# Four-block graph network: adjacency load moved ahead of the turned group's swap, loops from round 3, all instruction lists rewritten

## What is computed

```
h = relu(layernorm(x));  x = x + GCN0(h, adj)        # 2 layers
h = relu(layernorm(x));  x = x + ATT1(h, adj + adj)  # 12 heads of 32
h = relu(layernorm(x));  x = x + ATT2(h, adj)
h = relu(layernorm(x));  x = x + GCN3(h, adj)        # 2 layers
...
GCN0 layer: u = h·(Wl h)'/√384 above and on the diagonal, h·(Wr h)'/√384 below;
            a = exp(u)·adj / row sum;   h = relu(LN(a @ (Wlin h + b)))
ATT:        p = softmax(q k'·scale + bias) per head;   out = (p v) Wo' + bo
GCN3 layer: a = softmax(h h'/√384)·adj / row sum;
            ctx = upper(a) @ (Wl h) + diag(a)·(Ws h) + lower(a) @ (Wr h);   h = relu(LN(ctx))
```

## Time and profile before

| | |
|---|---|
| median of three executions | 2807.22 us (2806.8 to 2807.78) |
| the profiled execution | 2810.98 us |
| its span, first to last instruction | 2809.2 us |
| mean granted TensorE clock | 0.988 |
| TensorE busy | 2684.6 us, 96% |
| VectorE, GpSimd, ScalarE busy | 78%, 53%, 44% |
| a round in the loop: GCN0, attention, GCN3 | 49.6, 33.3, 52.3 us |

### The profile page before, as it was taken

One profiled execution on the slowest core, in us unless ns is written; L12 is line 12 of the kernel. 1 busy time (PEld: TensorE's weight loads), 2 busy tenths in 40 slices (PEclk: granted clock), 3 DMA queues, 4 the chain that ended last, 5 costly groups with the idle time before them and its releaser, 6 DMA issues.

```text
span 2809.2 us, 85451 instructions
## 1 busy us (share of the span) xinstructions
PE 2684.6 (96%) x33582; PEld 2472.3 (88%) x33582; DVE 2184.4 (78%) x4130; ACT 1224.2 (44%) x2007; POOL 1495.1 (53%) x2499
## 2 busy tenths in 40 slices
PE   7999999999988999999989999998999999999997
PEld 7988888888878899999888999998888888888886
DVE  5776777767767788888877888888677777777776
ACT  3333333333333454544544545454444444444443
POOL 2222222223214566665544666665677777777776
PEclk9999999999999999999999999999999999999999
DMA  5332232322323433333353333333132222222221
GB/s 162 103 108 84 84 106 63 113 77 89 103 76 108 142 121 124 125 123 121 108 158 111 121 122 127 121 122 119 55 96 80 71 90 78 71 90 78 72 84 48
DMA packets 224451, 284.59 MB, mean 101 GB/s; under 512 B 18256, under 2 KB 203984, under 8 KB 224336
## 3 DMA queue, kind: packets, MB, share of 16 engines
q1 hardware_dynamic: 224336, 282.96, 32.1%
HBM read 182.62 MB, written 100.27 MB: 101 GB/s over the span
## 4 chain that ended last, share of the span: by engine, by line
PE 37%; issue 22%; DVE 16%; POOL 15%; DMA 5%; ACT 3%; SPq 2%; POOLq 0%; DVEq 0%; ACTq 0%
PE ps L373 27%; POOL wide L1610 7%; PE ps L1435 3%; PE ps L1417 3%; PE ps L1450 2%; DMA adjin<-in_adj 2%; DVE heads L1308 2%; DVE wide L1299 2%; DVE heads L1316 2%; DVE heads L1322 2%; DMA bounce<-xin 1%; POOL small L722 1%; DVE wide L1332 1%; POOL wide L1595 1%; PE ps L1965 1%
## 5 line engine op out<-in xcount | busy, mean ns | idle before, releaser
L373 PE MATMUL ps<-w_hi,split 128*128 128x384 f32 x4608 | 1271.6, 346 | 26.3 <-ACT split L1673 17.6
L373 PEld LDWEIGHTS ps<-w_hi,split 128*128 128x128 f32 x4608 | 849.1, 191 | 56.9 <-issue 17.8
L373 PE MATMUL ps<-split,w_hi 128*128 128x256 f32 x4608 | 863.4, 283 | 14.8 <-DVE w_lo L450 11.1
L373 PE MATMUL ps<-w_lo,split 128*128 128x384 f32 x2304 | 787.6, 342 | 0.0
L373 PEld LDWEIGHTS ps<-split,w_hi 128*128 128x128 f32 x4608 | 721.3, 189 | 32.2 <-ACT w_hi L439 11.3
L373 PE MATMUL ps<-split,w_lo 128*128 128x256 f32 x2304 | 584.7, 283 | 0.0
L373 PEld LDWEIGHTS ps<-split,w_lo 128*128 128x128 f32 x2304 | 435.7, 189 | 17.3 <-issue 17.3
L373 PEld LDWEIGHTS ps<-w_lo,split 128*128 128x128 f32 x2304 | 439.0, 191 | 1.3 <-issue 1.2
L731 POOL TENSOR_TENSOR rstd<-mv,pos_half 128x2 f32<-128x2 f32 x64 | 59.0, 923 | 569.3 <-DVE mv L926 569.3
L1187 POOL TENSOR_TENSOR wide<-wide 128x192 f32<-128x192 f32 x256 | 213.4, 865 | 252.1 <-ACT wide L1253 252.1
L1610 POOL TENSOR_TENSOR wide<-wide,row 128x192 f32<-128x192 f32 x512 | 315.7, 652 | 1.5 <-ACT wide L1686 1.5
(11 more groups left out here) (145 smaller groups left out, 4473.8 us busy)
## 6 DMA issues: line engine op xcount, KB each, us to landing
bounce<-xin SPq DMA_DIRECT2D x127, 384.0 KB, 3.1
wide<-bounce SPq DMA_DIRECT2D x508, 96.0 KB, 2.2
x_after<-wide SPq DMA_DIRECT2D x96, 384.0 KB, 2.5
wide<-x_after SPq DMA_DIRECT2D x96, 384.0 KB, 3.3
xin<-x_after SPq DMA_DIRECT2D x190, 192.0 KB
xin<-in_x SPq DMA_DIRECT2D x66, 192.0 KB
wide<-in_x SPq DMA_DIRECT2D x32, 384.0 KB, 4.4
out<-wide SPq DMA_DIRECT2D x32, 384.0 KB, 2.8
```

What stands on the lines that cost most here:

```text
L373: mm = nc.tensor.matmul(out, t if tokens_stay else w, w if tokens_stay else t, start=(k == 0), stop=(k == len(pairs) - 1))
```

## The change

No instruction's work is changed, and each stage runs as often as before. Three things are:

1. In `turn(i)`, `adjacency(s, i)` is issued before `swap_quarters(s, i)`, not behind `tokens(s, i + 1)`. With it, its wait for GpSimd stands ahead of SyncE's waits for the turned group.
2. `MIXED` is 3: each phase's loop runs rounds 3 to 15, and the straight code is a round per phase shorter (TensorE's program has 2979 rows of instructions instead of 3693).
3. The loop orders, `BEGINNING`, `BETWEEN` and `ENDING` of all engines are rewritten. Line numbers behind the lists are 36 lower.

```
@@ -21,223 +21,187 @@
-MIXED = 4
+MIXED = 3
...
 GCN3_ORDERS = [
...
-    "agg_0.1'' on_1.0'' adj_0.0' stat.1' diag_1.0'' on_1.1'' w0_1.0'' w1_1.0'' adj_1.0' w0_1.1'' w1_1.1'' "
-    "adj_0.1' diag_1.1'' adj_1.1' agg_1.0'' w0_0.0' on_0.0' w1_0.0' diag_0.0' z.0'' on_0.1' agg_0.0' "
-    "agg_1.1'' diag_0.1' w0_0.1' stat.0 w1_0.1' z.1''",
+    "adj_0.0' agg_0.1'' stat.1' on_1.0'' diag_1.0'' w0_1.0'' w1_1.0'' adj_1.0' adj_0.1' on_1.1'' adj_1.1' "
+    "w0_1.1'' w1_1.1'' diag_1.1'' agg_1.0'' w0_0.0' on_0.0' w1_0.0' diag_0.0' z.0'' on_0.1' agg_1.1'' "
+    "agg_0.0' diag_0.1' w0_0.1' stat.0 w1_0.1' z.1''",
...
     def turn(i):
         for s in range(STREAMS):
             store_and_reload(s, i - 2)
+            adjacency(s, i)
             swap_quarters(s, i)
             tokens(s, i + 1)
-            adjacency(s, i)
```

More of the change, by code:

```diff
@@ L29 @@
 BEGINNING = [
[29 rows of a table removed]
[19 rows of a table added]
 ]
 GCN0_ORDERS = [
[5 rows of a table removed]
[5 rows of a table added]
     "u_0.0' agg_1.1'' lin0_0.0' aT_0.0' lin1_0.0'",
[1 row of a table removed]
[1 row of a table added]
     "aT_0.0' z_1.1'' z_0.0' ml_0.1' norm.0 mr_0.1' hT_1.0' soft_0.1' aT_0.1' z_0.1' ml_1.0' mr_1.0' norm.1",
     "split_1.1'' soft_1.0'' att_1.0'' sum_1.0'' lin_1.0'' split_0.0' agg_1.0'' ln_1.0'' gain.0'' soft_1.1'' "
[2 rows of a table removed]
[2 rows of a table added]
     "agg_0.1' stat.1 ln_0.1' beta.1'' out.1'' turn.1",
[1 row of a table removed]
[1 row of a table added]
 ]
 ATT_ORDERS = [
-    "q0.1'' q1.1'' q2.1'' k0.1'' k1.1'' v0.1'' v1a.1'' pt0.0'' v1bc.1'' pt1.0'' pt2.0'' k2.1'' pv.0'' "
-    "scores.1'' out0.0'' out1.0'' q0.0' q1.0' q2.0' k0.0' k1.0' v0.0' v1a.0' pt0.1'' v1bc.0' pt1.1'' pt2.1'' "
-    "k2.0' pv.1'' scores.0' out0.1'' out1.1''",
-    "q.1'' pt0.0'' hT.0' pt1.0'' pt2.0'' k.1'' pv.0'' out.0'' norm.0 exp.1'' q.0' pt0.1'' hT.1' pt1.1'' "
+    "q0.1'' q1.1'' q2.1'' k0.1'' k1.1'' v0.1'' v1a.1'' pt0.0'' v1b.1'' pt1.0'' v1c.1'' pt2.0'' k2.1'' pv.0'' "
+    "scores.1'' out0.0'' out1.0'' q0.0' q1.0' q2.0' k0.0' k1.0' v0.0' v1a.0' pt0.1'' v1b.0' pt1.1'' v1c.0' "
+    "pt2.1'' k2.0' pv.1'' scores.0' out0.1'' out1.1''",
+    "q.1'' pt0.0'' hT.0' pt1.0'' pt2.0'' k.1'' pv.0'' norm.0 out.0'' exp.1'' q.0' pt0.1'' hT.1' pt1.1'' "
     "pt2.1'' k.0' pv.1'' out.1'' norm.1 exp.0'",
-    "abs.0'' fac.0'' v.1'' turn.1' stat.0 hT.0' pv.0'' s.1'' soft.1'' abs.1'' fac.1'' turn.0 stat.1 v.0' "
-    "hT.1' pv.1'' s.0' soft.0'",
-    "bias.1'' bias.0' p.0'' stat.0 out.0'' xb.1'' p.1'' stat.1 xb.0' out.1''",
+    "abs.0'' fac.0'' turn.1' hT.0' v.1'' stat.0 pv.0'' s.1'' soft.1'' abs.1'' fac.1'' turn.0 stat.1 hT.1' "
+    "v.0' pv.1'' s.0' soft.0'",
+    "bias.1'' bias.0' p.0'' stat.0 xb.1'' out.0'' p.1'' stat.1 xb.0' out.1''",
 ]
 GCN3_ORDERS = [
[4 rows of a table removed]
[4 rows of a table added]
     "on_0.0'' soft_0.1'' swap_0.1'' tiny_0.1'' w0_0.1'' w1_0.1'' hT_1.0'' norm.0' on_0.1'' w0_1.0'' "
[5 rows of a table removed]
[5 rows of a table added]
     "split_1.0' w2_0.1' ln_1.1'' turn.0 agg_0.1' out.1'' ln_0.1' soft_1.0' stat.1 att_1.0'",
[3 rows of a table removed]
[3 rows of a table added]
 ]
```

## The result

The changed kernel takes 2791.49 us (median of four, 2788.18 to 2795.12) against 2807.08 us before (median of four). The ratio is 0.9944, 95% interval 0.9927 to 0.9962: 15.6 us faster, where 38 were forecast. The profiled execution has a span of 2793.2 us, 16.0 less than before, so the trace shows the whole difference.

A forecast was written before the change was run, and what follows sets the result against it. TensorE, busy 2684.6 of 2809.2 us, was taken as the bound. The terms −22 − 9 − 18 + 2 + 0 + 9 = −38 us took the median of 2807 to 2769 us, range 2748 to 2800 us.

The forecast's parts named there:

- GCN3 loop, −22: GCN3 loop: earlier adjacency load and new order save 1.6 us in each of 14 rounds; bounds −28 and −5.
- B and C: GCN3 loop: TensorE's layer-1 aggregation waits for POOL's w0 and DVE's w2 rows; 1.2 us per round together, −0.9 forecast.
- A: GCN3 loop: TensorE's product waits for ACT's swap split; the new POOL order takes 0.70 us out of its 0.93.
- rival (2): GCN3 loop: waits are replaced, DVE comes last for w2; −5 instead of −22, 2786 us; chance 0.09.
- (3): First passage gains nothing, the stagger trades one chain for another; 2787 us; chance 0.09.
- (4): Loops cost, straight code doesn't: each of four added loop rounds brings a 2.1 us gap; 2786 us; chance 0.05.
- Attention, −9: Attention straight code: two fewer groups with gaps save 7 us, separated blocks at the second passage 2 us.
- First passage, −18: GCN0 to attention: staggered streams cut 39.5 us of gaps and lost clock to 21 to 23; bounds −25 and 0.
- Steady loops, 0: GCN0 and attention loops each gain a round that ran as straight code; no change, within 3 us either way.
- Start, +9: Start: late first product, +1.6, and waits after the first two aggregations, about 5, plus half clock; bounds +4 and +13.
- Third passage +2, end 0: Attention to GCN3 costs +2 us (−5 to +7); the last aggregations at the end stay, 0.
- Slower rival (5): GCN3: POOL's masks, now first, delay everything behind if the adjacency is late; about 2820 us at 7.3 us; chance 0.08.

The follow-up runs named there:

- e3: The changed kernel with DVE's out of stream 0 put back behind the normalise ln_0 in GCN3; 2792.61 us.
- e15: The kernel before with the early adjacency load and DVE's out of stream 0 moved ahead of ln_0 in GCN3; 2789.6 us, ratio 0.9917.
- e6: The changed kernel with rounds 3 and 4 of both attention phases written out as straight code; 2808.45 us.
- e11: The kernel before, late load and old orders kept, with only MIXED = 3, so loops start from round 3; 2802.87 us, ratio 0.9981.
- e1: The kernel before with one edit, the adjacency load issued ahead of the swap; 2778.36 us, ratio 0.9892.
- e12: The kernel before with the early adjacency load and POOL's GCN3 order as changed; 2791.4 us, ratio 0.9926.
- e5: The changed kernel with DVE's GCN0 order as before, straight code set to match; 2783.31 us, ratio 0.9909.
- e2: The changed kernel with the adjacency load put back behind the tokens' load; 3054.75 us, ratio 1.0877.

## Why the prediction was wrong

The miss of 22 us is as large as the error of one term, the GCN3 loop. The errors of the others cancel: the start and the GCN0 loop (5.3 and 4.3 us) and the first passage (4.7) came out dearer than forecast, the attention loops (6.5), the second and third passage and the end (2.3, 2.7, 2.5) cheaper. That is luck.

**GCN3 loop, −22: failed, at its second step.** That POOL's wait for the late adjacency is the cause of B and C held: the load alone takes 1.45 us off a round, against 1.6. The failing step is "of B and C together −0.9, since I don't know that the reordered DVE list keeps all of it", and the 0.70 for A. I priced the load on the old lists and treated the new lists as at worst a small deduction. They replaced A, B and C by a wait for the normalise (1.14 per round) and one for the split (0.52), and the round came out at −0.19. (The 0.70 for A came from a power moved ahead. That isn't what ended A: in e3 it is back at 1.14 per round with that power still ahead, and in e15, with the old place of the power, it is gone. It goes where hT waits instead.) The bound of −5 and rival (2), the waits are replaced and DVE comes last, had this, though DVE comes last with the normalise and the split and not with w2; its sign, a round of 52 with DVE as the releaser, is what the trace shows. At 2786 it is, with (3) and (4), 5 us from the result, and I gave it 0.09, with the argument that DVE idles where it waits for POOL. DVE's idle time says nothing of the order in which DVE comes to a piece of work, nor of what its instructions do to POOL's. The prediction said of A that POOL's second power leaves the chain; it did not look at which DVE instruction would now stand ahead of the normalise, and run beside the first.

**Attention, −9: right** in place and size for the second passage, −11.3. The price per group was too high (3.4; 1.4 to 2.1 by e6), the number of gaps closed too low: 4 rather than 2. `MIXED` alone gives it all (e11, −11.5 in its trace); the 2 us for the separated blocks show in no run.

**First passage, −18: size.** −13.3. The gaps that I had walked were there, a little longer (1.00 and 1.23 us at the last aggregations but one, 1.56 for the key copy, 1.73 for u, 2.91 at the pt transposes), and the clock is 0.90 in the middle, with 41.66 us of work, where over 44 and over 0.93 had been named as the sign. That the stagger of the streams made the gain isn't shown: no run has it alone. `MIXED` alone makes this passage 5.4 us shorter (e11), the early load alone 1 to 7 (e1, e12 to e15), and if the two add, the stagger has 1 to 7 of the 13.3 us.

**Steady loops, 0, within 3 either way: wrong in both** (+4.3 and −6.5). GCN0 lost 0.48 per round, to DVE's order (e5); attention gained 0.37 per round, where its TensorE had idled 0.2 to 0.4 in 50 us. No idle is left there:

```profile
1000.00:1050.00 50.00, 50.00 (x949) 48.79 (x951) 43.17 (x51) 25.54 (x37) 29.72 (x44) 1.00 0.39 125
```

I had the lists' differences before me and judged from TensorE's 0.2 to 0.4 us of idle that nothing could change. It bounds neither way. GCN0 lost more than it had idled, and attention gained twice its idle: over eight rounds (266.1 us before, 263.1 after) the idle fell by 1.5 us and the busy time of the same 4704 matmuls by another 1.5. Neither `MIXED` alone nor the load alone changes that round (33.24 to 33.34 us in e1 and e11), so the gain is that of the new attention lists; which word of them, no run shows.

**Start, +9: size.** +14.3, of which the forecast gaps are as said and 2.3 us of wait and some 2 of half clock were missed. **Third passage +2, end 0:** −0.7, within its bounds, and −2.5.

**Slower rival (5): didn't occur;** e2 shows what it would have cost. **Rival (4): no.** The time lies inside the range, 2748 to 2800 us, but the gain is 15.6 us where 38 were called likeliest.

## What to carry to other kernels

Price an edit on the lists that will run, not on those that ran: when a change moves one transfer and reorders everything, the transfer's gain can be had alone (here some 30 us of median for one line) and the orders must pay for themselves, stretch by stretch. Compare the two kernels by the start of the n-th group of a kind on the bound engine; the table says at once which lists to keep from which. Here the kernel put together so is 39 us under the changed one, though two of its parts missed by 9 and 7 us and cancelled. A small idle share of the bound engine in a steady loop says little: here one loop lost more than it had idled, and another gained twice as much, half of it out of the engine's busy time.

## What the runs showed of the hardware

- POOL's power on 128x2 takes 0.70 us, and 1.3 to 1.5 us when DVE's two-operand `out` (128x768, 0.95 us) has started before it or within 0.03 us after it: 29 of 64 with the new order. Where the power starts 0.07 to 0.10 us ahead of `out`, both take their usual time: 15 of 64 before. I had not expected it to be paid twice per round, nor that the time would hardly change when it was taken away (e3).
- A mask load that leaves behind the swap and the tokens again costs 263 us (e2), some 18 us in each of 13 rounds and the passage before them: where an in-order engine takes a piece of work first in its round, a late transfer costs its lateness in each round, and the clock falls too (0.86 in a window of the loop that is else at 1.00).
- The small matmuls of attention in code that runs once meet gaps with no releaser, in the second passage before seven of them, 14.6 us together; the same groups in a loop have none in 21, and two rounds more of such code in each attention phase cost 17 us by the medians (e6). What the engine lacks in these gaps no row shows.
